# Turning split keys and queries with DMA transposes on the SP queue instead of TensorE transposes and ScalarE copies

## The reference

```python
x  = L0_attn_x                                   # (8, 1024, 512) float32
xn = layernorm(x)
# attention: 16 heads of 64, two "null" keys/values per head, causal, ALiBi slopes
q, k = l2norm(xn2 @ Wq) * q_scale, l2norm(xn @ Wk) * k_scale      # xn2: a second layernorm with norm_g, norm_b
sim  = 8.0 * q @ k.T + slope * (-|distance|)                       # causal mask
out  = softmax(sim) @ v ;  attn = out @ Wout
# the ffn half picks 8 // 16 = 0 tokens for each of its heads, so nothing is gathered, and what is left is:
ffn = layernorm(xn) * ln_g + ln_b
return x + attn + ffn
```

## Time and profile before

| | |
|---|---|
| median of 3 runs | 3886.16 us (3885.91 to 3892.84) |
| the profiled execution | 3888.84 us, of which its span is 3886.7 us |
| mean granted TensorE clock | 0.933 |
| busy: PE, DVE, ACT, POOL | 88%, 84%, 73%, 52% of the span |
| TensorE transposes L1055 | 2048, 178.6 us busy |
| ScalarE copies L459 | 256, 260.9 us busy |
| DMA traffic | 21 GB/s in the mean |

### The profile page before, as it was taken

One profiled execution on the slowest core, in us unless ns is written; L12 is line 12 of the kernel. 1 busy time (PEld: TensorE's weight loads), 2 busy tenths in 40 slices (PEclk: granted clock), 3 DMA queues, 4 the chain that ended last, 5 costly groups with the idle time before them and its releaser, 6 DMA issues.

```text
span 3886.7 us, 97861 instructions
## 1 busy us (share of the span) xinstructions
PE 3410.9 (88%) x35857; PEld 2291.0 (59%) x35857; DVE 3246.1 (84%) x8403; ACT 2830.7 (73%) x5453; POOL 2006.9 (52%) x2052
## 2 busy tenths in 40 slices
PE   1689989898998989889988998989989899898998
PEld 0356666565665656656665666656656566665665
DVE  6788888788887888888887888888888788887886
ACT  2477777677777778777787777777777677777776
POOL 2564455645556445554447445474454744556443
PEclk7789999999999999999999999989999899999999
DMA  3000000000010000100001001010000000000000
GB/s 129 21 15 2 21 21 31 20 2 23 18 37 15 2 23 26 34 10 2 29 23 39 2 4 34 23 31 2 15 26 29 23 2 23 18 34 12 2 2 23
DMA packets 41335, 82.39 MB, mean 21 GB/s; under 512 B 5792, under 2 KB 5792, under 8 KB 40352
## 3 DMA queue, kind: packets, MB, share of 16 engines
q1 hardware_dynamic: 36864, 67.13, 5.5%
q10 hardware_dynamic: 4000, 9.02, 0.6%
HBM read 59.36 MB, written 16.78 MB: 20 GB/s over the span
## 4 chain that ended last, share of the span: by engine, by line
PE 41%; DVE 24%; POOL 15%; issue 12%; ACT 7%; DMA 0%; ACTq 0%; POOLq 0%; DVEq 0%
DVE PS L780 5%; PE PS L969 5%; PE PS L970 5%; PE PS L971 5%; POOL RN L641 5%; PE PS L955 4%; DVE PL L850 4%; DVE Q2T L877 4%; PE PS L990 3%; PE PS L991 3%; PE PS L1032 2%; POOL QKB L634 2%; POOL STR L645 2%; DVE QKB L914 2%; ACT TOK L477 2%
## 5 line engine op out<-in xcount | busy, mean ns | idle before, releaser
L442 ACT ACTIVATE PR<-PS,BT,SC 128x512 f32<-128x512 f32 (+3 forms) x1536 | 1024.0, 667 | 360.0 <-PE PS L993 318.2
L780 DVE CUSTOM_DVE_ANT_0 PS<-PS,STR 128x512 f32<-128x512 f32 (+3 forms) x1536 | 834.4, 566 | 107.7 <-PE PS L955 97.7
L447 ACT ACTIVATE PH<-PR 128x512 f16<-128x512 f32 (+3 forms) x1536 | 804.0, 523 | 48.7
L850 DVE TENSOR_TENSOR PL<-PR,PH 128x512 f16<-128x512 f32 (+3 forms) x1152 | 692.5, 601 | 2.4 <-ACT PH L447 2.1
L641 POOL TENSOR_TENSOR RN<-SS,HALF 128x8 f32<-128x8 f32 x256 | 422.8, 1652 | 522.8 <-DVE SS L863 520.4
L969 PE MATMUL PS<-WH,XT 128*128 128x384 f16 x2048 | 671.3, 328 | 18.6 <-DVE QKB L801 18.6
L1022 PE MATMUL PS<-AR,PH 128*128 128x66 f16 x4608 | 612.7, 199 | 74.2 <-ACT PH L447 40.0
L970 PE MATMUL PS<-WL,XT 128*128 128x384 f16 x2048 | 669.7, 327 | 0.0
L971 PE MATMUL PS<-WH,XT 128*128 128x384 f16 x2048 | 669.6, 327 | 0.0
L593 POOL TENSOR_TENSOR PL<-PR,PH 128x512 f16<-128x512 f32 x384 | 449.1, 1169 | 423.2 <-ACT PH L447 416.5
L955 PE MATMUL PS<-AR 128*128 128x512 f16 (+3 forms) x1536 | 542.6, 353 | 137.6 <-DVE MX L780 91.4
(11 more groups left out here) (178 smaller groups left out, 7364.8 us busy)
## 6 DMA issues: line engine op xcount, KB each, us to landing
XW<-in_L_attn_x SPq DMA_DIRECT2D x128, 256.0 KB, 2.6
ACC<-in_L_attn_x SPq DMA_DIRECT2D x64, 256.0 KB, 2.6
out<-ACC SPq DMA_DIRECT2D x64, 256.0 KB, 2.0
AR<-in_L_attn_Wkv ACTq DMA_DIRECT2D x1, 4096.0 KB, 20.4
AR<-in_L_attn_Wq ACTq DMA_DIRECT2D x1, 2048.0 KB, 11.3
ACC<-in_L_attn_Wout ACTq DMA_DIRECT2D x1, 2048.0 KB, 25.1
LG<-in_L_ffn_ln_g ACTq DMA_DIRECT2D x1, 256.0 KB, 5.6
LB<-in_L_ffn_ln_b ACTq DMA_DIRECT2D x1, 256.0 KB, 5.8
```

The costliest lines, as they stand in the source:

```text
L442: e.activation(PR[:, n % 3, 0:wide], PS[:, n % 2, 0:wide], ACT.Exp, bias=BT[:, 2 * (u % NP) + h, kt - 4 * qc + 4:kt - 4 * qc + 5], scale=S ...
L447: e.activation(PH[:, n % 4, 0:wide], PR[:, n % 3, 0:wide], ACT.Copy).then_inc(s_ph, 1)
L780: e.tensor_tensor_reduce(out=r[:, 0:n], in0=r[:, 0:n], in1=ST[:, h, o:o + n], scale=1.0, scalar=LOW, op0=ALU.add, op1=ALU.max, accum_out=M ...
L850: e.tensor_tensor(PL[:, n % 3, 0:wide], PR[:, n % 3, 0:wide], PH[:, n % 4, 0:wide], ALU.subtract).then_inc(s_pl, 1)
```

## The change

The eight TensorE transposes and the ScalarE copy of a group go. In their place SP issues four DMA transposes, one for each of the two queries and two keys, straight from `TOK` to `KQ`, in slot 4g+10 (one slot earlier). The VectorE copy to `K2` moves from slot 4g+11 to 4g+12. The PSUM ring has one user less. The single semaphore `s_kq` becomes four, one for each group number, that count 64 for a unit.

```diff
-W_TP = [4 * g + 11 for g in range(4)]
+W_TP = [4 * g + 10 for g in range(4)]
+W_K2 = [4 * g + 12 for g in range(4)]
...
-        for u, g in due(s, W_TP):
-            take("tp", u, g)
...
+        def kq_done(e, u, last):
+
+            for g in range(last + 1):
+                e.wait_ge(s_kq[g], 64 * (u + 1))
...
+                for u, g in due(s, W_TP):
+                    i = 4 * u + g
+                    w.wait_ge(s_hi, 2 * i + 2)
+                    w.wait_ge(s_lo, 2 * i + 2)
+                    if u > 1:
+                        w.wait_ge(s_o, 4 * (u - 1))
+                    for j in range(4):
+                        e.dma_start_transpose(KQ[:, u % 2, j, 256 * g:256 * g + 256].rearrange("p (a n) -> p a n", a=2),
+                                              TOK[:, j, :, :].rearrange("p a n -> p (a n)")).then_inc(s_kq[g], 16)
...
-                for u, g in due(s, W_TP):
-                    w.wait_ge(s_tp, 4 * u + g + 1)
-                    if u > 1:
-                        w.wait_ge(s_o, 4 * (u - 1))
-                    e.activation(KQ[:, u % 2, :, 256 * g:256 * g + 256],
-                                 rb("tp", u, g).bitcast(F16).rearrange("p (j c) -> p j c", j=4), ACT.Copy).then_inc(s_kq, 1)
...
                 for u, g in due(s, W_HI):
                     i = 4 * u + g
                     w.wait_ge(s_t1, i + 1)
-                    w.wait_ge(s_tp, i)
+                    if i:
+                        w.wait_ge(s_kq[(i - 1) % 4], 64 * ((i - 1) // 4 + 1))
...
-                for u, g in due(s, W_TP):
-                    w.wait_ge(s_kq, 4 * u + g + 1)
+                for u, g in due(s, W_K2):
+                    kq_done(w, u, g)
...
-                w.wait_ge(s_kq, 4 * u + qt // 2 + 1)
+                kq_done(w, u, qt // 2)
...
-                for u, g in due(s, W_TP):
-                    i = 4 * u + g
-                    r = rb("tp", u, g).bitcast(F16)
-                    bank_free(w, "tp", u, g)
-                    w.wait_ge(s_hi, 2 * i + 2)
-                    w.wait_ge(s_lo, 2 * i + 2)
-                    for j in range(4):
-                        for a in range(2):
-                            ins = e.transpose(r[:, P * (2 * j + a):P * (2 * j + a) + P], TOK[:, j, a, :], IDH[:, :])
-                    ins.then_inc(s_tp, 1)
```

More of the change, by code:

```diff
@@ L245, in fused_block @@
         s_proj, s_qev, s_kvev, s_sq, s_ss, s_rn = (mk("s_" + z) for z in ("proj", "qev", "kvev", "sq", "ss", "rn"))
-        s_t1, s_t2, s_hi, s_lo, s_tp, s_kq, s_k2 = (mk("s_" + z) for z in ("t1", "t2", "hi", "lo", "tp", "kq", "k2"))
+        s_t1, s_t2, s_hi, s_lo, s_k2 = (mk("s_" + z) for z in ("t1", "t2", "hi", "lo", "k2"))
+        s_kq = [mk(f"s_kq{g}") for g in range(4)]
         s_str, s_s, s_mx, s_nm, s_m, s_c = (mk("s_" + z) for z in ("str", "s", "mx", "nm", "m", "c"))
@@ L273, in bank_free @@
                 e.wait_ge(s_m, 2 * (2 * u + i) + 1)
-            elif what == "tp":
-                e.wait_ge(s_kq, 4 * u + i + 1)
             elif what == "ntp":
@@ L1039, in _ @@
                     bank_free(w, "nm", u, qc)
-                    w.wait_ge(s_kq, 4 * u + 2 * qc + 2)
+                    kq_done(w, u, 2 * qc + 1)
                     for q in range(4):
```

## The result

The changed kernel takes 4120.18 us in the median of four runs (4111.62 to 4121.69), the kernel before 3886.43 us beside it. The ratio is 1.0593 with an interval of 1.0575 to 1.0611, so 230 us more. The forecast was 58 us less. The time lies near the upper end of the range, where rival 1 stands: transposes that follow one another on SP more slowly than assumed.

A forecast was written before the change was run, and what follows sets the result against it. DVE bounds the preparation and PE the longer stretch behind it. Removal -79 us, late group 3 +4, transposes behind stores +11 and late loads +6 make -58, a median of 3828 us; range over all 3740 to 4130.

The forecast's parts named there:

- rival 1: TOK and group 3's pieces: DMAs don't overlap, gain gone at 0.82 us spacing, 4093 us at 1.3; chance 0.27.
- D: Time from the end of lo to the fourth transpose's landing: taken as 5.1 us, bounded by 3.4 and 10.9.
- The allowances: D before anybody waits longer: pieces of group 1 5.28 us, group 3 5.04; hi of group 2 6.35, group 3 6.77.
- It costs DVE what it did: VectorE's copy to K2, one slot later: claimed to take the same DVE time, so no added cost.
- it waits for nothing: Copy to K2 in its later slot, 6.5 us after lo in group 2: claimed not to wait at 5.1 us.
- The removal: TensorE transposes and ScalarE copies taken away: claimed to save 79 us together.
- ScalarE's part: ScalarE's copies L459, which hold up the K2 copy on DVE: claimed to be worth 40.1 us.
- rival 2: PE's clock falls with less work, low part growing into PE's stretch: 109 us, 3937 us; chance 0.10.
- TensorE term: TensorE's transposes L1055 on the chain: 4.91 us in each of eight batches, claimed to save 39.3 us.
- The other 180 us of ACT's copies: ScalarE copies beside PE and DVE work: claimed to be worth nothing when removed.
- Rival 3: Preparation: a second path, GpSimd's steps, is as long, so only PE's 39 us count; 3868 to 3886 us; chance 0.08.
- signs for being right: Landing 4 to 5.3 us after lo, hi hardly waiting, copy's wait gone, PE bounding its stretch, removed work off the chain.

The follow-up runs named there:

- e13: Changed kernel with the same bytes turned by two 128x512 transposes in a group instead of four of 128x256, three tiles laid out anew: 3910.33 us, 1.0046.
- e2: Changed kernel with only the keys' two transposes in a group, the queries' half of KQ left zero: 3909.18 us, 1.0046.
- e3: Changed kernel with each transpose cut into two of 128x128, eight issues in a group for the same bytes: 5369.05 us in one run.
- e4: Changed kernel with transposes in slot 4g+9, the queries' issued after hi and the keys' after the first lo: 3911.91 us, 1.0058.
- e1: Changed kernel with no transposes at all, KQ filled with zeros, K2 copy still in slot 4g+12: 3886.94 us, 0.9998.
- e6: Kernel before with only the VectorE copy to K2 moved to slot 4g+12: 3929.55 us, 1.0102.
- e5: As e1, no transposes and KQ zeros, but with the K2 copy back in slot 4g+11: 3833.12 us, 0.9852.
- e12: Kernel before without ScalarE's copies, KQ zeros, TensorE's transposes kept: 3850.98 us, 0.9903.
- e15: As e13, with the K2 copy in slot 4g+11, the queries' transpose issued after hi, the keys' after the first lo: 3849.82 us, 0.9887.
- e11: Kernel before with the queries turned by DMA, issued after hi, and the keys still on TensorE and ScalarE: 3881.13 us, 0.9988.

## Why the prediction was wrong, by its own steps

**The step that failed: the spacing in D.** "I take the spacing of the line with the dearest repeated issue, 0.63 us". It is 1.29 us: 1.25 for the issue and 0.04 between two. The landing was 2.4 and not 3.2, so D is 3 x 1.29 + 2.4 = 6.3 us undisturbed, 6.2 in the rows above, and 6.7 to 6.95 in the mean, where 5.1 was taken. The bounds, 3.4 and 10.9, held it; the choice between them, at the low end, was wrong. The plain DMAs that were taken as the nearest rows issue in 0.45 to 0.63 us, and nothing in them showed that a transpose takes twice that. That the loss follows from the spacing and the number of issues is shown by e13, e2 and e3.

**The allowances priced the loss about right, and that is partly luck.** By the prediction's own rule, with D = 6.8 a unit loses (6.8 - 5.04) + (6.8 - 5.28) = 3.3 us, 210 us in 64 units. From e4 to the change the measured step is 1.0593 - 1.0058 = 5.35%, 208 us. But e4 is not inside every allowance: a quarter of its groups land later than 5.04 us, and its pieces wait 137.5 us in 93 groups. And the rule has no term for the pieces of group 2, which wait 152.2 us in the change, a third of all that pieces wait, and none for the copy. So the sum agrees while its terms do not. Further out the rule falls short: for e3 it gives D = 7 x 1.27 + 2.3 = 11.2 us and 16.5 us in a unit, 1056 us over e1, and 1482 were measured. There the copy waits 1214.1 us, which the rule doesn't count, and the granted clock is 0.810; which of the two makes up the rest was not separated.

**"It costs DVE what it did" was wrong, and so was "it waits for nothing".** The copy one slot later runs beside GpSimd's subtraction and multiplication: 333 ns became 569 in the change. e6 prices the move at 40 us on the kernel before, e5 against e1 at 57. I had checked what the copy waits for in its new slot and not what runs beside it. The copy also had to wait in the change (188.3 us). Its allowance of 6.5 us was read from group 2 and a mean slot, but VectorE reaches the copy of group 3 sooner, as e1 shows, where nothing has to land (lo, then the copy):
```profile
2023.95 0.41 DVE L876 TENSOR_TENSOR Q2T<-QKB,TOK 128x256 f16<-128x256 f32 x1
```
```profile
2028.88 0.27 DVE L855 COPY AR<-AR 64x512 f16<-64x512 f16 x1
```
That is 4.5 us after lo (7.2 in group 2 of the same unit), so even at D = 5.1 the copy would have waited there. In the change it waits in all 64 units in group 3.

**The removal was mis-sized.** 79 us were forecast, 57 measured (e5). ScalarE's part was right in size, 38 for 40. TensorE's was 20 for 39. The granted clock in e5 is 0.917 against 0.937 in e12 and 0.933 before, that is, some 635 us at 1.2 GHz against 485 and 520: in these runs it is lower where TensorE has less to do. That fits rival 2, with a loss that is a part of the TensorE term and not the 109 us priced there. Whether the clock explains all of the missing 19 us was not isolated. ("The other 180 us of ACT's copies" should read 213, 260.9 less 48.1; it was counted at nothing, so no sum changes.)

**The sum, with measured terms.** Removal -57, copy's slot +57, four transposes issued early +23, the same four behind both lo steps +208: 231 us, where 230 were measured. The terms are differences of ratios that end at the change itself, so the sum must come out and only the split is a finding: e1 to e5 shows the second, e4 and e1 the third, e4 and the change the fourth.

**The rivals.** Rival 1 came true: the spacing is over its tipping point of 0.82 us, and the pieces of groups 1 and 3 and hi wait as it said, though those of groups 0 and 2, which it left out, wait 211.8 of the 464.7 us. Its 4093 us at a spacing of 1.3 are 27 us under the measurement. It did not price the copy's slot, and it took a removal of 79 us and a landing of 3.2 us. The Trainium skill, VectorE: DVE Perf Modes, advises TensorE where PSUM will do (its section "Rules for kernel authors"), and so spoke against the change. The sign agrees for the change and not for e15, which is faster than TensorE's transposes with ScalarE's copy. The 1309 ns for a block in its section "The three transpose paths" are near the time of an issue of any of the three sizes here, so with four issues in a group the eight blocks in a line, an estimated 10.5 us, did not come about; with eight issues, in e3, D is 11.2 us. Rival 3 didn't come true: ScalarE's copies alone are worth 38 us, by e12.

**Signs.** Those named for a wrong forecast came: L482 (L475 before) and L962 (L955 before) wait for the DMA, over 1 us each time in the mean, and issues lie over 0.82 us apart. The lower clock at the start of PE's stretch did not come: it is 1.00 there (2150 to 2160 us), and the 0.92 and 0.91 lie in the preparation. Of the signs for being right, the wait for ScalarE's copy is gone, neither it nor a TensorE transpose is on the chain, and PE stays the bound of its stretch; the landing, 6.2 us or more after lo, lies outside the 4 to 5.3 that were named.

**What stays open.** 82 of the 1024 issues take over 1.4 us, 61 us more than the median would give; the one at 2121.56 stands behind a store, and for the rest no cause was found. How much of the 208 us goes through the granted clock, 0.901 in the change, was not separated; a low mean clock alone doesn't make the loss, since e13 has 0.909 and loses 18 us. And e11's small gain, above.

## What to carry to other kernels

Before work is moved to a DMA queue, price the issue of that very kind of instruction on its queue, count the instructions between the last input and the first user, and make them few and wide: here the same bytes in half the instructions gave back 213 of 230 us. Split what a transfer waits for, so that the part whose input is early goes early. And when a step moves by a slot, look at what the other engines run beside its new place: a VectorE copy of 0.27 us took 1.24 beside a GpSimd subtraction.

## What the runs showed of the hardware that was not expected

- A DMA transpose from SBUF to SBUF holds SP for 1.23 us at 128x128, 1.25 at 128x256 and 1.25 at 128x512, and lands 2.3 to 2.5 us after its issue begins (all in the median).
- A float16 copy of 64x512 on VectorE took 0.27 us by itself and 1.24 beside a GpSimd subtraction, ending 0.15 us after it; beside GpSimd's power operation it took 0.28.
- Taking transposes away from TensorE went with a lower mean granted clock: 0.937 with them (e12), 0.929 with half of them (e11), 0.917 without (e5).
